# A selective scan laid out as 8 channels by 16 states, with rows broadcast from DRAM

## The reference

```
x = x + attn_a(layernorm(x))     # 16 heads of 8, 64 features a head, causal
x = x + ffn(layernorm(x))        # hidden width 352, values rounded in blocks of 16
x = x + mixer(layernorm(x))
x = x + ffn(layernorm(x))
```

```
dA  = exp(dt[..., None] * A)                     # A = -exp(A_log), 256 x 16
dBu = (dt * u)[..., None] * Bm[:, :, None, :]
h_t = dA_t * h_(t-1) + dBu_t                     # h_0 = 0, per channel and state
y_t = sum over n of h_t[d, n] * C_t[n]           # then y + u * D
```

## Time and profile before

| | |
|---|---|
| median of three runs | 1375.67 us |
| the profiled execution | 1378.12 us, its span 1376.4 us |
| PE busy | 1126.2 us (82%) |
| DVE busy | 985.4 us (72%) |
| ACT busy | 937.2 us (68%) |
| POOL busy | 484.4 us (35%) |
| mean granted TensorE clock | 0.91 |
| DMA | 41.12 MB, mean 30 GB/s |

### The profile page before, as it was taken

The page is one execution under the profiler, slowest core; times in us unless marked ns, Lnnn a source line. Parts: engine busy times, 40 slices in busy tenths (PEclk is TensorE's granted clock), DMA queues, the critical chain, the costliest instruction groups (busy, mean ns, idle before and its releaser), DMA issues. The chain is left out here.

```text
span 1376.4 us, 17231 instructions
## 1 busy us (share of the span) xinstructions
PE 1126.2 (82%) x5421; PEld 621.8 (45%) x5421; DVE 985.4 (72%) x1472; ACT 937.2 (68%) x1829; POOL 484.4 (35%) x457
## 2 busy tenths in 40 slices
PE   3875887899789988899789988999889987747844
PEld 1343344544544454545544454545544454415423
DVE  1645559886897689876897689877897688645733
ACT  3543779677885769576885869586886768467711
POOL 3110216531454116621454126511543126405623
PEclk8986899999999999999999999999999999967865
DMA  2000002100110002100120102100110002001200
GB/s 73 1 8 0 19 14 62 39 1 32 41 60 9 32 1 77 31 2 31 46 54 8 33 10 68 31 24 10 48 53 1 32 24 61 17 31 38 62 0 8
DMA packets 31403, 41.12 MB, mean 30 GB/s; under 512 B 4617, under 2 KB 14674, under 8 KB 31314
## 3 DMA queue, kind: packets, MB, share of 16 engines
q1 hardware_dynamic: 31314, 40.02, 10.0%
HBM read 37.65 MB, written 2.36 MB: 29 GB/s over the span
## 5 line engine op out<-in xcount | busy, mean ns | idle before, releaser
L624 POOL TENSOR_TENSOR read<-state,c_row 128x1024 f32<-128x1024 f32 x128 | 300.4, 2358 | 237.7 <-DVE state L1159 68.5
L1159 DVE TENSOR_TENSOR_SCAN state<-decay,bank 128x512 f32<-128x512 f32 x256 | 295.7, 1203 | 57.5 <-PE bank L1476 48.0
L1492 PE MATMUL bank<-read,ident 128*128 128x512 f32 x512 | 258.7, 634 | 1.1 <-POOL read L624 1.1
L1476 PE MATMUL bank<-ident,drive_by_token 128*128 128x128 f32 x1024 | 161.6, 294 | 95.7 <-DVE state L1159 85.6
L728 ACT ACTIVATE drive_by_token<-dtu_t,b_t 128x256 f32<-128x256 f32 x512 | 217.3, 500 | 1.0 <-PE bank L1476 0.9
L665 POOL TENSOR_SCALAR expf<-expf 128x512 f32<-128x512 f32 x104 | 69.2, 665 | 379.6 <-ACT expf L704 379.0
L1476 PEld LDWEIGHTS bank<-ident,drive_by_token 128*128 128x128 f32 x1024 | 119.5, 148 | 162.3 <-issue 104.8
L716 ACT ACTIVATE decay<-dt,neg_a 128x510 f32<-128x510 f32 x256 | 169.7, 714 | 16.4 <-DVE state L1159 16.3
L1169 DVE TENSOR_TENSOR s_sb<-bank,causal 128x512 f32<-128x512 f32 x128 | 88.2, 689 | 112.5 <-PE bank L1430 112.5
L1417 PE MATMUL bank<-znt,omega 128*128 128x512 f32 x256 | 145.8, 653 | 10.2 <-ACT sqf L707 10.2
L704 ACT ACTIVATE expf<-bank,minus_s,root2s 128x512 f32<-128x512 f32 x128 | 99.3, 776 | 69.2 <-PE bank L1417 66.0
(11 more groups left out here) (236 smaller groups left out, 1694.6 us busy)
## 6 DMA issues: line engine op xcount, KB each, us to landing
c_row<-c_rows SPq DMA_DIRECT2D x128, 256.0 KB, 3.2
xa<-x_dram SPq DMA_DIRECT2D x8, 256.0 KB, 3.6
out_dram<-x SPq DMA_DIRECT2D x8, 256.0 KB, 2.3
omega<-omega_t_dram SPq DMA_DIRECT2D x1, 512.0 KB
c_rows<-xdbl SPq DMA_DIRECT2D x8, 32.0 KB, 1.6
wqkv<-w_qkv_t_dram SPq DMA_DIRECT2D x1, 192.0 KB
state<-w_down_dram SPq DMA_DIRECT2D x1, 176.0 KB, 2.5
state<-w_gate_dram SPq DMA_DIRECT2D x1, 128.0 KB, 2.0
```

The source lines that it names most:

```text
L624: pool.tensor_tensor(read[:, s % STATE_BUFFERS], state[:, s % STATE_BUFFERS], c_row[:, s % C_BUFFERS].unsqueeze(1).broadcast_to([P, DT, TO ...
L1159: dve.tensor_tensor_scan(state[:, s % STATE_BUFFERS, c], decay[:, s % 2, c].rearrange("p b t -> p (b t)"), bank[:, DRIVE_BANK + c], 0.0, A ...
L1476: last = pe.transpose(bank[:, DRIVE_BANK + c, t * P:(t + 1) * P], by_token[:, s % DRIVES, t, c * P:(c + 1) * P], ident[:])
L1492: last = pe.matmul(bank[:, 6 + k], ident[:], read[:, s % STATE_BUFFERS, k], start=(s == 0), stop=(s == STATES - 1))
```

## The change

A scan step is no longer one state for 256 channels but a "span" of two tiles, and a tile is 8 channels x 16 states on the 128 partitions. There are 32 tiles, so 16 spans; the number and size of the scans stay.

- dt and dt*u are stored to DRAM (16 stores of 32 rows a group) and loaded back with each channel's row repeated on 16 partitions: per span one DMA for dt (into `dt_rows`, four buffers) and one for dt*u (into `state`, eight buffers), 512 KB each. B and C rows are loaded once per group, each row on 8 partitions.
- ScalarE writes the decay into PSUM banks 4 and 5, one instruction per tile; each tile's bank has to wait for that tile's scan of the span before. The transposes, `drive_by_token`, `dtu_t` and `b_t` are gone.
- GpSimd multiplies `state` in place by `b_rows` (`drive`, four spans ahead of the scan), VectorE scans in place, GpSimd multiplies in place by `c_rows` (`read_out`).
- TensorE sums over states with 0/1 matrices of 32 columns (`pick`), into 32 partitions of banks 6 and 7, from slot 2 on in `SUMS`.
- `vector_rest`, with its waits, is gone. Two `tensor_scalar` of VectorE become `scalar_tensor_tensor` with a tensor operand. dt and dtu are made in slot 10 in place of 12, over half_x and tanh_x. Some semaphores are merged.

```diff
-STATE_BUFFERS = 3
+STATE_BUFFERS = 8
+DT_BUFFERS = 4
+DECAY_BANK = 4
+LEAD = 4
...
+            def store_dt(group, values, dram, done, stored_in):
+
+                sp.wait_ge(done.sem, done.at(group, 1))
+                sp.wait_ge(state_done.sem, state_done.at(group, 0))
+                per = WIDE // CHANNELS
+                for k in range(DT):
+                    rows = dram[per * k:per * (k + 1)].rearrange("q d g t -> g (q d) t")
+                    for g in range(P // WIDE):
+                        sp.dma_start(rows[g], values[WIDE * g:WIDE * (g + 1), k]).then_inc(
+                            stored_in.sem, 16)
...
+            def load_dt(group, s):
+
+                sp.wait_ge(dt_stored.sem, dt_stored.at(group, DT_STORES))
+                sp.wait_ge(decay_done.sem, decay_done.at(group, 2 * (s + 1 - DT_BUFFERS)))
...
+            def load_dtu(group, s):
+
+                sp.wait_ge(dtu_stored.sem, dtu_stored.at(group, DT_STORES))
+                sp.wait_ge(y_ps.sem, y_ps.at(group, s + 1 - STATE_BUFFERS))
...
-            def vector_rest(turn, k):
-
-                new, mid = turn.new, turn.mid
-                if turn.has_new and k == 0:
-                    pool.wait_ge(norm_a.var.sem, norm_a.var.at(new, 1))
...
+            def in_place(span, rows):
+
+                return pool.tensor_tensor(span, span, rows[:].unsqueeze(1).broadcast_to(
+                    [P, 2, TOK]), ALU.mult)
+
+            def drive(group, s):
+
+                landed = state_loaded[s % STATE_BUFFERS]
+                pool.wait_ge(bc_loaded.sem, bc_loaded.at(group, 2))
+                pool.wait_ge(landed.sem, landed.at(group, s // STATE_BUFFERS + 1))
+                in_place(state[:, s % STATE_BUFFERS], b_rows).then_inc(drive_done.sem, 1)
...
+                for e in range(2):
+                    scanned = half_done if e == 0 else state_done
+                    act.wait_ge(scanned.sem, scanned.at(gb, s))
+                    act.activation(
+                        by_sequence(bank[:, DECAY_BANK + e])[:, :, 1:],
+                        by_sequence(dt_rows[:, s % DT_BUFFERS, e])[:, :, 1:], ACT.Exp,
+                        scale=neg_a[:, tile_of(s, e):tile_of(s, e) + 1]).then_inc(
+                            decay_done.sem, 1)
...
+                dve.wait_ge(drive_done.sem, drive_done.at(gb, s + 1))
+                for e in range(2):
+                    span = state[:, s % STATE_BUFFERS, e]
+                    dve.wait_ge(decay_done.sem, decay_done.at(gb, 2 * s + e + 1))
+                    dve.tensor_tensor_scan(span, bank[:, DECAY_BANK + e], span, 0.0, ALU.mult,
+                                           ALU.add).then_inc(
...
+                k, q = divmod(s // 2, WIDE // CHANNELS)
+                for e in range(2):
+                    g = 2 * (s % 2) + e
+                    last = pe.matmul(bank[WIDE * g:WIDE * (g + 1), 6 + k], pick[:, q],
+                                     state[:, s % STATE_BUFFERS, e], start=(q == 0),
+                                     stop=(q == WIDE // CHANNELS - 1))
```

More of the change, by code:

```diff
@@ L865, in mixer_early @@
                     ffn_ht(ffn_b, old, 0)
-                if turn.has_mid and k == 14:
-                    for h in range(DT):
-                        act.wait_ge(dtu_t_ps.sem, dtu_t_ps.at(mid, h + 1))
-                        act.activation(
-                            dtu_t[:, 2 * h:2 * h + 2].rearrange("p t c -> p (t c)"),
-                            bank[:, 4 + h], ACT.Copy).then_inc(dtu_t_done.sem, 1)
             def mixer_rest(turn, k):
@@ L1701, in body @@
                         gates(ffn_a, mid, 0)
-                    if turn.has_old and k + 1 < STATES:
-                        drive(old, k + 1)
                     if turn.has_mid and k == 6:
@@ L1722, in body @@
                 if turn.has_old:
[L1723 to L1725 removed]
+                    sum_states(old, SPANS - 1)
                 if turn.has_new:
```

339 lines of the change are left out of this document (149 added, 190 removed).

## The result

The changed kernel takes 1596.6 us (median of four runs, 1595.0 to 1598.9), the kernel before 1376.5 in the same session; the ratio is 1.159, with a 95% interval of 1.156 to 1.162. Slower was forecast and the time lies in the range of 1420 to 1645, but 42 us above the 1555 that I predicted. Terms were wrong in opposite directions, so the sum looks better than its parts: the six full first stages came out 28 us shorter than forecast, the six second stages 39 us longer, and turn 1, turn 8 and the last turn together 29 us longer.

The account below looks back on a forecast made before the run. VectorE bounds the first stage, TensorE is busiest in the second. Six turns of 18 + 6 give 144; with turns 1, 8 and the last, 180 on 1378.12: 1558, predicted 1555 us, range 1420 to 1645.

Parts of the forecast that it names:

- Exclusion on VectorE and GpSimd: Whichever engine starts first holds the shared SBUF ports for its whole instruction; VectorE's 18 sharing first-stage instructions exclude GpSimd.
- Rows 3 to 5: Profile rows before the change: VectorE's qk, guard and clip slowed beside GpSimd instructions, read as proof of shared ports.
- The rival in which nothing is shared (1438): Slow pairs were chance; first stage bound by GpSimd's own 76.2 us, +2, tail +6; 1438 us, chance 0.13.
- Term A: Steady first stage: twelve added GpSimd multiplications plus port collisions lengthen it from 74.6 to 92.7 us, +18.
- The ledger: First-stage slots laid out one behind the other, VectorE and GpSimd each in order; read-out 15 ends at 92.7 us.
- The two sums below it: First stage's lower sums: 76.2 us with nothing shared, 88 us with shared ports if GpSimd never starves.
- VectorE's 12.1 us of shared instructions: Eighteen first-stage VectorE instructions on hidden tile, input tile, qk and guards; added to GpSimd's 71.8 us, giving 83.9.
- Term B: End of second stage: dt and dtu pass through DRAM, GpSimd waits for rows with a clip queued behind; +6 us.
- The last turn, +10: Last turn's first stage: GpSimd 46.11 + 12 x 2.36 = 74.4 us in 69.0, with collisions +10 us.
- TensorE's clock (1653): Less TensorE work lowers its clock, lengthening FFN links: first stage +25, tail +12; 1653 us, chance 0.13.
- The change on ScalarE and in PSUM: Scans stay 1.20 us, exponentials 0.71; exponentials waiting for the scan to leave the bank cost nothing, up to 1 us a slot.

Follow-up runs that it names:

- before_no_waits: The kernel before without GpSimd's waits for VectorE's other work of the slot, nothing else changed: 1430.7 us.
- short_read_outs: The changed kernel with GpSimd's read-out multiplication on 8 of each 512 columns, the rest of the product by C left out: 1503.7 us.
- sums_twice: The changed kernel with every TensorE matmul that sums states issued twice: 1593.6 us.
- first_drives_on_vector: The changed kernel with drives 0 to 3 of each group on VectorE, each right before its scan: 1577.9 us.

## Why the prediction was right in sign and off in its terms

That the total came within 42 us is in part luck: 28 us too much for the first stages stand against 68 too little for everything else.

*Exclusion on VectorE and GpSimd, the deciding mechanism: right.* Rows 3 to 5 were no chance. Thirteen VectorE instructions of turn 4's first stage are stretched by over 0.1 us, five before. before_no_waits shows its price without any added work, in the kernel before; short_read_outs shows the stage falling back when half of GpSimd's multiplications go. VectorE's excess makes 10.3 of the stage's 13.4 us. How the rest divides between exclusion and a GpSimd that is simply fuller is not shown, since short_read_outs takes both away. The rival in which nothing is shared (1438) is refuted by the same runs.

*Term A, the first stage, +18 within +2 to +29: the mechanism held, the size was 13.4.* The ledger had VectorE end scans 4, 8 and 12 at 24.7, 51.7 and 78.3 us; turn 4 has 24.1, 49.5 and 74.3, and read-out 15 ends at 88.6 in place of 92.7. The two sums below it held (GpSimd 71.8 forecast, 75.2 less 4.8 of stretch measured). What was too dear is the mutual part: I let GpSimd pay for VectorE's 12.1 us of shared instructions in full, and it lost 4.8; VectorE did most of the waiting, 15.7 us, 10.3 more than before.

*Term B, the tail, +6 within -6 to +12: the mechanism held, the size was 12.5.* The wait on rows before drive 0 with a clip behind it was there, 12.8 us long, and is worth 6 to 7 of the 12.5 by the two runs that take it away. Two inputs of the term were too cheap. The sixteen stores' issue took 8.5 us in turn 4 (0.59 us each for dt's eight, one of them 1.51) and 7.4 to 7.6 in five of the eight groups, where the sum took 6.4. The rows' pace was 4.3 to 4.5 us a pair against 3.1 from the earlier trace rows. From dtu to its first rows I had 11.3 us (641.7 to 653) and turn 4 has 13.3. The term had no entry for the rest: span 15's sum stands before scores 0, and dt and dtu before VectorE's mask 11 (both read from the masks above, not run apart). It also left out what TensorE's lower clock adds in the tail, about 2 us.

*The last turn, +10: wrong, 24.6.* I added twelve multiplications to GpSimd's 46.11. But without attention there is no work to cover the rows: drives 1, 2 and 3 also fall behind scan 0, at the pace of the loads (1441.43, 1445.95, 1450.47), and read-out 0 is queued behind drive 3 and began 13.3 us after scan 0 did. That makes fifteen multiplications, not twelve, and GpSimd stood 6.6 us for rows between them. Turns 1 and 8 carry the same uncovered transfers.

*TensorE's clock (1653): refuted for the first stage, in part right for the tail.* It fell as that rival said, to 0.68 in turn 4's first stage. There it cost nothing that can be seen: the stage is 100 us long at 0.91 and 78 us at 0.72 in other kernels, and sums_twice raised the clock to 0.82 without a change. Behind mask 11 of the second stage the low clock goes with 2.1 us a turn in first_drives_on_vector, whose tail has no multiplication of GpSimd in it. My forecast put this at nothing.

*The change on ScalarE and in PSUM: right for the steady turns.* Scans 1.200 us, exponentials 0.685. Each exponential waits for the scan that empties its bank, and it is hidden in the steady stages: the scans waited 36.7 us for them over the whole run, 15.9 of those before the last group's scan 0, where the exponential itself waited for the rows of dt, and 19.7 in the last turn.

What stays open: what the later first mask and the earlier dt are worth when run apart, why TensorE's clock falls in the tail, and why the kernel with a second multiplication and no waits is 6 us a stage longer than the count explains.

## What to carry to other kernels

Before giving work to an idle engine, ask which instructions of the busiest engine it will hold up: in the kernel before, the waits that kept GpSimd away from VectorE were worth 51 us by themselves, although they look like idle time in the profile. An in-order queue with a wait on a transfer in it delays everything behind it; put the work that others wait for ahead of it. Cost the partial turns apart, since their transfers have no cover. And test a low clock stage by stage: here it cost the first stage nothing that showed, and the end of the second some 2 us a turn.

## What the runs showed of the hardware that I had not expected

Four stores of 256 KB, each with its target cut in four outer pieces, ran at 89 GB/s and a DMA share of 0.24, and the first load behind them went out 14.0 us after the first of them; with the same bytes in the order of the source's rows it was 4.1. The number of issues saved (16 to 4) was worth less than the pace lost. That the outer pieces set the share is inferred from these two layouts alone.

Two bursts with the DMA engines full moved different amounts: 334 GB/s at a share of 0.98 in the kernel before, and 244 at 1.04 here, where each of 512 KB is read 16 times over from 32 KB in pieces of 4 KB. Which of the two properties it is no run shows.

GpSimd's multiplication has a fixed part: 128x1024 takes 2.36 us and two of 128x512 take 2 x 1.27, 0.18 more.

The same stretch of TensorE's work, mask 11 to mask 12, took 2.49 us at a granted clock of 1.00 and 4.33 at 0.50, with TensorE busy from end to end in both.
